# Normalising the residual rows one chunk an iteration instead of four at once

## What is computed

```python
x = _layernorm(x + _L0_attn_ref(x, ...))   # a state-space layer (Mamba-like)
x = _layernorm(x + _L0_ffn_ref(x, ...))    # a mixture of experts
```

## Time and profile before

| | |
|---|---|
| median of 3 runs | 784.41 us (782.98 to 786.55) |
| profiled execution, its own time | 785.97 us |
| its span, first to last instruction | 784.2 us |
| granted TensorE clock, mean | 0.924 of full speed |
| busy: TensorE, VectorE, GpSimd, ScalarE | 658.8, 608.7, 497.6, 444.4 us |
| share of the chain that ended last: PE, issue, ACT, DVE | 44%, 13%, 11%, 11% |

### The profile page before, as it was taken

The page is one execution under the profiler, slowest core; times in us unless marked ns, Lnnn a source line. Parts: engine busy times, 40 slices in busy tenths (PEclk is TensorE's granted clock), DMA queues, the critical chain, the costliest instruction groups (busy, mean ns, idle before and its releaser), DMA issues.

```text
span 784.2 us, 14802 instructions
## 1 busy us (share of the span) xinstructions
PE 658.8 (84%) x4299; PEld 557.2 (71%) x4299; DVE 608.7 (78%) x1838; ACT 444.4 (57%) x1225; POOL 497.6 (63%) x545
## 2 busy tenths in 40 slices
PE   5987888999999999999999998886697877776840
PEld 4865676787787787787778887675587877665730
DVE  4899889999999999999999887337236342588875
ACT  4875777868767867877876754411113111335645
POOL 1144454887787787777887875566565656555652
PEclk9899999999999999999999999897799989898875
DMA  8541111121111221111221127123323222555436
GB/s 299 190 135 41 43 39 31 64 59 55 61 51 58 65 58 55 52 62 59 58 62 48 35 85 247 48 61 90 82 72 85 82 83 80 163 146 158 139 95 214
DMA packets 62639, 70.76 MB, mean 90 GB/s; under 512 B 10335, under 2 KB 45285, under 8 KB 62304
## 3 DMA queue, kind: packets, MB, share of 16 engines
q1 hardware_dynamic: 52656, 52.79, 23.2%
q0 software_dynamic: 8608, 16.87, 6.3%
q10 hardware_dynamic: 1296, 0.16, 0.1%
HBM read 48.55 MB, written 23.01 MB: 91 GB/s over the span
## 4 chain that ended last, share of the span: by engine, by line
PE 44%; issue 13%; ACT 11%; DVE 11%; another core or an unknown queue 4%; DMA 2%; SPq 2%; POOL 0%; DVEq 0%; ACTq 0%; POOLq 0%
PE bank L793 6%; PE bank L728 5%; PE bank L748 5%; PE bank L802 4%; PE bank L860 4%; ACT x L909 3%; PE bank L776 2%; PE bank L847 2%; ACT rows L1001 2%; PE bank L857 2%; PE bank L809 2%; PE bank L761 2%; PE bank L864 2%; DVE xbcT_area L1117 2%
## 5 line engine op out<-in xcount | busy, mean ns | idle before, releaser
L602 POOL DMA_INDIRECT returned<-xT,slots_in x141 | 142.7, 1012 | 102.5 <-DVE xT L1419 62.2
L661 POOL DMA_INDIRECT dispatched<-rows,row_u x128 | 147.2, 1150 | 31.6 <-issue 31.3
L1117 DVE SCALAR_TENSOR_TENSOR xbcT_area<-raw,conv_w,xbcT_area 128x512 f32<-128x512 f32 x162 | 125.5, 776 | 2.5 <-ACT xbcT_area L975 2.4
L728 PE MATMUL bank<-xT 128*128 128x128 f32 x564 | 85.0, 308 | 30.3 <-issue 12.8
L920 ACT ACTIVATE raw<-bank 128x512 f32<-128x512 f32 (+1 forms) x71 | 39.9, 588 | 117.2 <-remote 78.9
L728 PEld LDWEIGHTS bank<-xT 128*128 128x128 f32 x564 | 79.0, 221 | 34.6 <-issue 19.7
L1419 DVE COPY xT<-bank 128x512 f32<-128x512 f32 (+1 forms) x36 | 24.4, 678 | 101.1 <-remote 87.6
L748 PE MATMUL bank<-xbcT_area,raw 128*128 x564 | 83.3, 301 | 16.8 <-issue 16.0
L748 PEld LDWEIGHTS bank<-xbcT_area,raw 128*128 128x128 f32 x564 | 76.9, 214 | 20.6 <-issue 20.6
L1125 DVE TENSOR_TENSOR_SCAN decay_area<-decay_area,ident_heads 128x512 f32<-128x512 f32 x64 | 87.3, 1365 | 0.0
L946 ACT ACTIVATE zs<-bank 128x256 f32<-128x256 f32 x64 | 24.3, 379 | 110.0 <-PE bank L761 110.0
(11 more groups left out here) (232 smaller groups left out, 1531.0 us busy)
## 6 DMA issues: line engine op xcount, KB each, us to landing
decay_area<-decay_rows SPq DMA_DIRECT2D x64, 256.0 KB
slots_in<-dispatched SPq DMA_DIRECT2D x141, 64.5 KB
hid<-returned SPq DMA_DIRECT2D x18, 256.0 KB
xT<-xT_dram SPq DMA_DIRECT2D x8, 512.0 KB, 8.1
x<-x_dram SPq DMA_DIRECT2D x8, 512.0 KB, 7.9
out_dram<-x SPq DMA_DIRECT2D x16, 256.0 KB
xT<-returned SPq DMA_DIRECT2D x14, 256.0 KB
returned<-xT,slots_in POOLq DMA_INDIRECT x141
```

The lines of the kernel that those rows point to most:

```text
L602: e.indirect_dma_start(returned, bass.IndirectOffsetOnAxis(ap=slots_in[sb_][:, n, D:ROW].bitcast(U32), axis=0), slots_out[b][:, n * P:(n + ...
L661: e.indirect_dma_start(dispatched, bass.IndirectOffsetOnAxis(ap=row_u[t % 2][:, m:m + 1], axis=0), rows[t % 3][:, k, c4, :], None).then_in ...
L728: mm = e.matmul(bank[:, off:off + P], w1_now[b][:, k * P:(k + 1) * P], slotsT[gr % len(slotsT)][:, n % 4 * P:(n % 4 + 1) * P], start=True, ...
L1117: e.scalar_tensor_tensor(o, r[:, n:n + W], conv_w[:, k, TAPS - 1 - n:TAPS - n], o, ALU.mult, ALU.add).then_inc(S["conv"])
```

## The change

`normalise` takes the chunks of a tile that it is to do. The call for a whole tile leaves iteration 4t + 11. In its place one chunk is done in each of the iterations 4t + 12 to 4t + 15, behind the block of iteration 4t + 11 and ahead of the copy L1009. The call in the tail (`"x2"`) still does all four.

```diff
-            def normalise(t, signal):
-                for c in range(4):
+            def normalise(t, signal, chunks=range(4)):
+                for c in chunks:
                     e.activation(x[:, 4 * t + c, :], x[:, 4 * t + c, :], ACT.Identity, scale=rstd[:, t, 0, c:c + 1], bias=shift[:, t, 0, c:c + 1]).then_inc(S[signal])
...
                     on.wait_ge("xn", 5 * t + 4)
                     e.activation(buf[:, 1, :, 0:D], buf[:, 0, :, 0:D], ACT.Copy).then_inc(S["xn"])
-                    normalise(t, "x1")
+                t, c = divmod(i - 12, 4)
+                if 0 <= t < NT:
+
+                    normalise(t, "x1", (c,))
                 t = due(i, 12)
                 if t is not None:
                     on.wait_ge("xnT", t + 1)
```

## The result

The changed kernel takes 773.26 us (median of four runs, 769.31 to 774.18) against 783.69 us before (four runs, 782.7 to 786.55): ratio 0.9858, 95% interval 0.9823 to 0.9893. The profiled execution took 774.18 us (span 772.4) against 785.97 us (784.2). The forecast was 775.7 us, in a range of 772 to 781.

What follows compares the result with a forecast made beforehand. TensorE sets the loop's pace, VectorE hardly behind, ScalarE's late entry stalling it once a tile. Gains of 1.5 + 1.2 + 5.8 + 0.2 = 8.7 us take 784.41 to 775.7 us, range 772 to 781.

Steps and rivals of the forecast that it cites:

- The two stalls: In iteration 12, TensorE waits 0.72 us at L782 and 0.21 us at L816 because ScalarE enters late; both go.
- The added L909: One L909, some 0.39 us, ending each of iterations 12 to 15 delays nothing; at worst 0.39 us a tile.
- What TensorE could give: L782's stalls 5.5 us, L816's 2.4, first tile 1.5 and 0.2 at 481 to 486 us: 9.6 us.
- What VectorE lets through: Eight tiles from 208 us: VectorE, next in line, passes on 4.9 to 6.6 us; the middle, 5.8, taken.
- the long scans of 2.08 and 2.36 us: VectorE scans right after two of its longest waits, usually 1.22 us; an earlier VectorE may be spared them.
- The sum: Whole kernel: 1.5 + 1.2 + 5.8 + 0.2 = 8.7 us gained, giving 775.7 us as median.
- Before 208 us: First tile gives 1.5 us; of 1.3 us in the two tiles after it, 1.2 us comes through.
- The rest of the span: Behind 437 us work follows the loop by semaphores, so the loop's gain is passed on whole.
- The rival that it takes the gain back: Behind 467 us, waits for DRAM loads and tables lose half or all the gain: 780 to 784; chance 0.08.
- The first rival: VectorE's 0.64 us margin per tile caps the gain at 7.6 us, or 3.9 with longer scans (780.5); chance 0.15.
- The second: VectorE's scans collide with GpSimd's products on a shared port: 3.8 us slower, 788.2; chance 0.05.
- The row at 338.15 us: VectorE scan of 2.36 us with a GpSimd product begun at 338.26 under it, taken to agree with port locking.

Runs made afterwards that it cites:

- the lighter tap: Changed kernel with the convolution's last VectorE tap on 128 of 512 columns, result not the reference's: 768.58 us, ratio 0.9777 to the unchanged kernel with full taps.
- the repeated run: The changed kernel run once more, unaltered, on another chip: 773.54 us against 783.89 before there, ratio 0.9844.
- the narrow products: Changed kernel with GpSimd's products L593 and L649 cut from 64 to 8 columns a head, result not the reference's: 767.66 us (one run).
- the lighter tap without the change: Kernel before the change, its last VectorE convolution tap on 128 of 512 columns: 782.18 us against 786.61 with full taps, ratio 0.9944.

## Why the prediction was right

- **The two stalls.** Right in place and size. L946 starts 0.67 us behind L761 (296.20 - 295.52 = 0.68 expected); all of the 0.72 and 0.21 us went in each of the shown tiles.
- **The added L909.** Taken at nothing. One more instruction beside each cost 0.15 us in eight tiles and nothing in nine, so the first one was as good as free. That the entry has only some tenths of margin is borne out too, since 1.5 us more brings the stalls back.
- **What TensorE could give.** This term was too small. The prediction had 6.6 us for the eight tiles; with VectorE out of the way (the lighter tap) the change gives 7.85 us there. The stalls by start distances were read rightly, but with the full tap two of the eight tiles had a smaller one (L782 1.12 and 1.35 us behind L776), where with the lighter tap all eight have 1.49 to 1.58 us. That makes 0.6 of the 1.2 us; where the rest comes from isn't shown.
- **What VectorE lets through.** 5.8 us were taken, the middle between 4.9 and 6.6. Measured are 6.65 us from rank matmul to rank matmul, 5.6 us between places where VectorE stands alike, and 5.8 us over nine tiles (5.9 in the repeated run). So the size was right, and VectorE does hold back a part. The agreement is in part luck: no row fixed a point between the two ends, and the upper end was too small. VectorE's idle time in the eight tiles fell from 8.0 to 2.8 us, most of it its wait at L1143. The lead was carried, as supposed, but it was spent once, 1.05 us in eight tiles, and then TensorE waited 1.16 us. And the long scans of 2.08 and 2.36 us were spared: the longest is now 1.64 us.
- **The sum.** Up to the thirteenth rank matmul the prediction had 1.5 + 1.2 + 5.8 = 8.5 us; measured are 457.06 - 448.63 = 8.4 us, and 9.05 in the repeated run. The median fell by 10.4 us and not by 8.7. From the thirteenth rank matmul to the end it was 327.1 us before and 323.8 and 326.2 us after, in all twelve profiles 323.5 to 331.3. No term can be named for the 1.7 us more.
- **Before 208 us.** 2.7 us expected, 2.7 measured in the profile; but the agreement hides two things. Of the 2.7 us, 0.28 lie ahead of the first tile's L776, where nothing was changed. And counted from there the gain is 2.4 us in the profile and 4.6 us in the repeated run. The stretch between the first and second rank matmul took 31.2 us in one profile of the same code and 28.25 in the other, and the clock differs (the columns as above):

```profile
119.00:125.00 6.00, 3.18 (x18) 2.92 (x18) 5.52 (x10) 4.68 (x12) 3.61 (x6) 0.70 0.13 46
125.00:131.00 6.00, 5.80 (x23) 4.12 (x22) 5.17 (x12) 2.81 (x9) 1.84 (x2) 0.73 0.12 44
```

```profile
121.00:127.00 6.00, 3.17 (x27) 2.95 (x25) 6.00 (x10) 4.65 (x12) 3.61 (x5) 1.00 0.14 46
127.00:133.00 6.00, 5.67 (x35) 4.20 (x34) 5.90 (x21) 5.12 (x15) 2.56 (x3) 1.00 0.19 44
```

The profile of the kernel before lies between, so that its share of this term can't be told from the clock's:

```profile
121.36:151.25 29.89, 26.41 (x149) 20.34 (x147) 28.65 (x75) 21.95 (x64) 19.58 (x21) 0.94 0.16 45
```

- **The rest of the span.** Passing the gain on whole fits: the part behind the twelfth rank matmul has its own scatter of 8 us and no trend by the edits. The rival that it takes the gain back is out for half or all of it; a part of 1 or 2 us could not be seen.
- **The first rival** (VectorE takes the gain) is out in size: the loop kept more than its 4.9 us, and no scans were added. Its premise held: nine tiles gave 5.8 us, which is the 0.64 us a tile that it named. **The second** (scans collide) named a real cause, shown by the narrow products, but the number of long scans did not rise, 20 before and 19 and 18 in the two profiles after. That it can rise with a shift is shown by the lighter tap without the change, with 27.

## What to carry to other kernels

A burst on an engine with 25% idle time can still set the pace, if the first thing behind it empties a PSUM bank that the busy engine needs at once. Look at the distance between two starts on the bound engine in a disturbed iteration and in a quiet one; the shown idle time leaves part of a stall out. To cure it, move the burst to an iteration with idle time behind it; here spreading it added nothing that the runs show. And an engine that waits 0.6 us a tile for the bound one follows by about that much; a lead between its result and its reader can be spent once. So measure a gain between places where both engines stand alike, or the spent lead is taken for a gain.

## What the runs showed of the hardware

A wait of 2.8 us of TensorE (from the first tile's rank matmuls to L844) was followed by a granted clock of 0.70 and 0.73 over 12 us in one execution of the changed kernel, and by 1.00 in another with the same wait; between them lie 2.95 us. In the first, the eight matmuls of L860 right behind the wait took 1.91 us instead of 1.06, so for a part of the 12 us the clock was at the lower of its levels, 1.2 GHz. The same code differs by that much, and the gain before 208 us is uncertain by it.

VectorE's scan of two tensors takes 1.22 us alone and 1.63 us in the place where it meets GpSimd's products, which themselves take 1.05 and 1.52 us there (0.60 at their shortest). With products an eighth as wide no scan is long, but the loss has moved. Here are a scan and a product of the narrow kernel that meet, and a product that meets no scan:

```profile
277.53 1.26 DVE L1130 TENSOR_TENSOR_SCAN decay_area<-decay_area,ident_heads 128x512 f32<-128x512 f32 x1
277.68 1.15 POOL L593 TENSOR_TENSOR xend<-xdt,outof 128x32 f32<-128x32 f32 x1
...
271.92 0.23 POOL L593 TENSOR_TENSOR xend<-xdt,outof 128x32 f32<-128x32 f32 x1
```

The product that takes 0.23 us alone takes 1.15 us when it begins within the scan, and ends 0.04 us behind it. These rows agree with the exclusive lock that the Trainium skill describes (SBUF — State Buffer, "SBUF: two separate sides"), by which the one that starts second waits for the first. The row at 338.15 us, on which the prediction rests, does not agree in the order. There the scan starts first, and both products that begin within it take no longer than their shortest:

```profile
338.15 2.36 DVE L1125 TENSOR_TENSOR_SCAN decay_area<-decay_area,ident_heads 128x512 f32<-128x512 f32 x1
338.26 0.60 POOL L649 TENSOR_TENSOR state_kept<-state,whole 128x256 f32<-128x256 f32 x1
338.83 0.60 POOL L593 TENSOR_TENSOR xend<-xdt,outof 128x256 f32<-128x256 f32 x1
```

It was the scan that lost 1.14 us, about both products together. The first two starts are only 0.11 us apart and GpSimd's records are rough, so which of them the chip took first can't be told from these rows. Nor is it shown why the usual long scan loses 0.41 us, less than either product lasts.
